# One normalisation stage between two attentions: statistics in a stage of their own, the add on GpSimd and the normalising on VectorE

## The reference, cut to what matters

```python
h = _layernorm(x, axis=-1) * (1 + ca) + sa
x = x + ga * _L0_attn_ref(h, ...)
h = _layernorm(x, axis=-1) * (1 + cb) + sb      # this line
x = x + gb * _L0_ffn_ref(h, ...)
```

## Time and profile before

| | us |
|---|---|
| median of 3 runs (4648.97, 4651.31 and 4651.40) | 4651.31 |
| the profiled execution's own time | 4651.4 |
| its span in the trace | 4649.8 |
| PE busy, share of the span | 3990.6, 86% |
| DVE busy | 3415.0, 73% |
| ACT busy | 2530.9, 54% |
| POOL busy | 1182.0, 25% |

### The profile page before, as it was taken

One profiled execution on the slowest core, in us unless ns is written; L12 is line 12 of the kernel. 1 busy time (PEld: TensorE's weight loads), 2 busy tenths in 40 slices (PEclk: granted clock), 3 DMA queues, 4 the chain that ended last, 5 costly groups with the idle time before them and its releaser, 6 DMA issues. The chain is left out here.

```text
span 4649.8 us, 98758 instructions
## 1 busy us (share of the span) xinstructions
PE 3990.6 (86%) x39612; PEld 2306.0 (50%) x39612; DVE 3415.0 (73%) x5521; ACT 2530.9 (54%) x3374; POOL 1182.0 (25%) x881
## 2 busy tenths in 40 slices
PE   7999999499969789978875999999999999726995
PEld 4788888255545445554543322332333333614664
DVE  4677778688865478865587899999989886575544
ACT  2566666455534345534323667787888887203652
POOL 1000000577840178841141000000000000312554
PEclk9999999699989889999977999999999999757998
DMA  1000000223320023220045000000000000203443
GB/s 58 1 1 1 1 1 1 58 50 56 50 60 0 9 51 55 50 54 20 0 108 94 13 11 4 11 4 3 11 3 11 4 12 8 77 0 108 95 100 95
DMA packets 289596, 157.03 MB, mean 34 GB/s; under 512 B 214704, under 2 KB 281220, under 8 KB 289156
## 3 DMA queue, kind: packets, MB, share of 16 engines
q1 hardware_dynamic: 250612, 100.68, 10.8%
q0 software_dynamic: 13440, 20.98, 2.5%
q10 hardware_dynamic: 25136, 29.64, 2.0%
HBM read 72.72 MB, written 33.55 MB: 23 GB/s over the span
## 5 line engine op out<-in xcount | busy, mean ns | idle before, releaser
L2010 DVE TENSOR_REDUCE s_tops<-ps 128x2 f32<-128x1024 f32 (+3 forms) x1152 | 1250.7, 1131 | 153.9 <-PE ps L1896 113.8
L1979 ACT ACTIVATE s_weights<-ps 128x1024 f32<-128x1024 f32 (+3 forms) x1152 | 1093.7, 953 | 344.1 <-PE ps L1909 190.1
L1931 PE MATMUL ps<-s_weights,v_flat 128*32 128x256 f32 (+1 forms) x8704 | 691.2, 389 | 7.6 <-ACT s_o_t L1985 6.2
L1890 PE MATMUL ps<-keys,s_q 48*128 48x512 f16 (+3 forms) x2304 | 433.9, 374 | 56.2 <-DVE s_tops L2010 25.9
L1909 PE MATMUL ps<-s_q,keys 50*128 50x512 f16 (+3 forms) x2304 | 433.8, 373 | 49.3 <-DVE s_tops L2010 33.2
L428 PE MATMUL ps<-a_qt,a_kt 128*128 128x256 f16 x3072 | 373.6, 273 | 3.8 <-POOL s_ones L412 3.8
L2046 POOL CAST s_shift<-s_minus_top 128x16 f16<-128x16 f32 x32 | 6.3, 198 | 1438.5 <-DVE s_minus_top L2017 1438.5
L1909 PEld LDWEIGHTS ps<-s_q,keys 50*128 50x128 f16 x2304 | 112.1, 93 | 513.6 <-issue 247.1
L929 PE MATMUL ps<-la_wqkv,la_yt 128*128 128x512 f16 x1152 | 287.8, 397 | 68.7 <-DMA la_yt<-la_y_parts 61.2
L1008 ACT ACTIVATE w_all<-ps 128x1024 f32<-128x1024 f32 x124 | 127.6, 1029 | 389.8 <-PE ps L919 389.8
L428 PEld LDWEIGHTS ps<-a_qt,a_kt 128*128 128x128 f16 x3072 | 300.0, 98 | 39.5 <-POOL s_ones L412 4.2
(11 more groups left out here) (353 smaller groups left out, 7629.6 us busy)
## 6 DMA issues: line engine op xcount, KB each, us to landing
ex_w_whole<-in_L_ffn_w_dram ACTq DMA_DIRECT2D x16, 1024.0 KB, 7.2
qk_parts<-a_parts SPq DMA_DIRECT2D x64, 128.0 KB, 2.4
keys<-qk_parts SPq DMA_DIRECT2D x48, 128.0 KB, 4.8
s_q<-qk_parts SPq DMA_DIRECT2D x48, 128.0 KB, 4.4
w_all<-in_L_ffn_wqkv_dram SPq DMA_DIRECT2D x3, 1536.0 KB, 6.4
x<-in_x_dram SPq DMA_DIRECT2D x4, 1024.0 KB, 9.5
a_table<-in_rope_dram POOLq DMA_DIRECT2D x8, 512.0 KB, 5.5
heads_out<-s_o_now SPq DMA_DIRECT2D x32, 128.0 KB, 1.9
```

Source lines behind the costliest of these rows:

```text
L1890: mm = pe.matmul(m.ps[:, bank, 0:width], b.q[rows(half, KEY_PARTS * L1_DH), place % 2, pair, t * P:(t + 1) * P], m.keys[rows(half, KEY_PAR ...
L1931: mm = pe.matmul(m.ps[h * QUAD:(h + 1) * QUAD, OUT, begin:end], m.v_flat[:, first:first + QUAD], weights[:, a % 2, h, begin:end], start=(k ...
L1979: act.activation(weights[:, a % 2, 2 * pair:2 * pair + 2, skip:CHUNK], m.ps[:, bank:end + 1, skip:CHUNK], ACT.Exp).then_inc(s["exp"], 1)
L2010: dve.tensor_reduce(tops[:, u % 2, :, i % 2, t, c], m.ps[:, bank:end + 1, 0:width], AX.X, ALU.max).then_inc(s["max"], 1)
```

## The change

The statistics leave `transformer_input` for a stage of their own, `norm_statistics(nc, m, "n1")`, right ahead of it. In `transformer_input` ACT has no work left. DVE normalises each tile with one instruction (subtract the mean, multiply by `rstd`) and multiplies the chunk. POOL adds the row, behind all its constants. The ring has 2 chunks in place of 3. The lists of DVE and POOL are loops of four rounds with two chunks in each (`in_pairs`) in place of written-out code, and their waits count from a credit of 64 that each semaphore gets at the start (`credit`, `need`).

```diff
-    FIRST, SLOTS = TPC, 3
-        normed = ctx.enter_context(nc.sbuf_tensor("y0_normed", [P, SLOTS, TPC, D], F32))
-        minus = ctx.enter_context(nc.sbuf_tensor("y0_minus", [P, TILES], F32))
+        normed = ctx.enter_context(nc.sbuf_tensor("y0_normed", [P, 2, TPC, D], F32))
...
-            @block.scalar
-            def _(act):
-                for c in range(CHUNKS):
-                    if c < 2:
-                        act.wait_ge(s["minus"], c + 1)
-                    if c >= SLOTS:
-                        act.wait_ge(s["y"], c - SLOTS + 1)
-                    for j in range(TPC):
-                        t = c * TPC + j
-                        n = act.activation(normed[:, c % SLOTS, j, :], m.x[:, t, :], ACT.Identity, bias=minus[:, t:t + 1], scale=m.rstd[:, t:t + 1])
-                    n.then_inc(s["normed"], 1)
-
             @block.vector
             def _(dve):
-                statistics_on_vector(dve, m, stats, s)
-                for n, part in enumerate(parts):
-                    dve.wait_ge(s["rstd"], n + 1)
-                    dve.scalar_tensor_tensor(minus[:, part], m.mean[:, part], -1.0, m.rstd[:, part], ALU.mult, ALU.mult).then_inc(s["minus"], 1)
-                for c in range(CHUNKS):
-                    now = normed[:, c % SLOTS, :, :]
-                    dve.wait_ge(s["normed"], c + 1)
-                    dve.tensor_tensor(now, now, m.modb[:, 4:5, :].broadcast_to([P, TPC, D]), ALU.mult).then_inc(s["scaled"], 1)
-                    dve.wait_ge(s["scaled"], c + 1)
-                    dve.tensor_tensor(m.y[:, c * TPC:(c + 1) * TPC, :], now, m.modb[:, 3:4, :].broadcast_to([P, TPC, D]), ALU.add).then_inc(s["y"], 1)
+                credit(dve, s["normed"], s["scaled"])
+
+                def norm(c, u):
+                    need(dve, s["y"], c - 1)
+                    for j in range(TPC):
+                        t = bass.ts(c * TPC + j, 1)
+                        n = dve.tensor_scalar(normed[:, u, j:j + 1, :], m.x[:, t, :], m.mean[:, t], m.rstd[:, t], ALU.subtract, ALU.mult)
+                    n.then_inc(s["normed"], 1)
+                    need(dve, s["normed"], c + 1)
+                    dve.tensor_tensor(normed[:, u, :, :], normed[:, u, :, :], m.modb[:, 4:5, :].broadcast_to([P, TPC, D]),
+                                      ALU.mult).then_inc(s["scaled"], 1)
+
+                in_pairs(dve, CHUNKS, norm)
...
             def _(pool):
+                credit(pool, s["y"])
+
                 pool.memset(m.mask[:, :, :], 0.0)
                 pool.memset(band[:, :, :], 0.0)
                 pool.memset(spread[:, :, :], 0.0).then_inc(s["zeroed"], 1)
-                pool.wait_ge(s["var"], 1)
-                for part in parts:
-                    pool.tensor_tensor(m.rstd[:, part], m.rstd[:, part], m.minus_half[:, part], ALU.pow).then_inc(s["rstd"], 1)
                 pool.wait_ge(s["zeroed"], 1)
...
                 pool.memset(m.spread[0:1, :, :], 1.0)
+
+                def shift(c, u):
+                    need(pool, s["scaled"], c + 1)
+                    pool.tensor_tensor(m.y[:, bass.ts(c, TPC), :], normed[:, u, :, :], m.modb[:, 3:4, :].broadcast_to([P, TPC, D]),
+                                       ALU.add).then_inc(s["y"], 1)
+
+                in_pairs(pool, CHUNKS, shift)
...
+            norm_statistics(nc, m, "n1")
             transformer_input(nc, m, f)
```

More of the change, by code:

```diff
@@ L599, in transformer_input @@
     NEG = -1e30
-    FIRST, SLOTS = TPC, 3
     with ExitStack() as ctx:
-        normed = ctx.enter_context(nc.sbuf_tensor("y0_normed", [P, SLOTS, TPC, D], F32))
-        minus = ctx.enter_context(nc.sbuf_tensor("y0_minus", [P, TILES], F32))
+        normed = ctx.enter_context(nc.sbuf_tensor("y0_normed", [P, 2, TPC, D], F32))
         band = ctx.enter_context(nc.sbuf_tensor("y0_band", [P, 2, P], F32))
         spread = ctx.enter_context(nc.sbuf_tensor("y0_spread", [P, 2, P], F32))
-        stats = statistics_buffers(nc, ctx, "y0")
-        with stage(nc, "y0", "table_in", "w_in", "zeroed", "selected", "spread", "minus", "normed", "scaled", "y", *STATISTICS) as (block, s):
-            parts = slice(0, FIRST), slice(FIRST, TILES)
+        with stage(nc, "y0", "table_in", "w_in", "zeroed", "selected", "spread", "normed", "scaled", "y") as (block, s):
             @block.sync
```

## The result

The changed kernel takes 4677.99 us (median of 5 runs, 4671.59 to 4684.86), the kernel before 4651.4 (median of 5, 4648.97 to 4656.73). The ratio is 1.0056, 95% interval 1.0044 to 1.0069: slower, by 20 to 32 us. A repetition in another session gave 1.0047 (1.0035 to 1.0059). The prediction, 4671.5 us or +0.43%, had the sign and most of the amount, but the median lies 2.5 us above its range. With the repetition's 1.0047 it would have lain inside (4673.2 us), so the runs alone don't tell a growth of 0.43% from a somewhat larger one. The traces do.

A forecast was written before the change was run, and what follows sets the result against it. It took the uncovered normalising stage, bound by DVE's chain, as the limit: 0.7 us at the start plus 19.5 (42.4 for 22.9) gives +20.2, so 4671.5 us (+0.43%), range 4665 to 4675.5.

The forecast's parts named there:

- What bounds the stage: Normalising stage: barriers on both sides, no other work covers it, so each microsecond it grows is one of the whole time.
- The power and the second barrier: Stage start: power ends at 844.73, the second barrier takes 1.3 us, DVE's first normalising starts at 846.0.
- GpSimd ready for shift 0: Normalising stage: POOL's constants, queued ahead of the first row add, are done and that add starts at 856.0.
- the 0.9 of turns: Constants beside DVE's first two chunks: both take 0.9 of their summed work, 9.7 us for 10.8, as in the stage before.
- Rival (a): Normalising stage: POOL's constants don't wait for DVE, POOL ready at 852.0, kernel time 4667.6 us; chance 0.10.
- the prediction's other sum: Constants by the exclusive port lock: each select and cast excludes DVE fully, POOL ready at 856.8, kernel time 4672.3 us.
- The pace from there on: Normalising stage after the first row add: six chunks (2 to 7) at 4.58 us each, 27.5 us, ending at 888.4.
- The stage as a whole: Normalising stage: its end goes from 868.17 to 888.4, +20.2 us, with the 0.8 of barrier behind it unchanged.
- The rival without exclusion (c): Normalising stage: DVE and POOL don't exclude each other, +3.5 us, kernel time 4654.9 us, within 0.2%; chance 0.07.
- the one with full turns (b): Chunk loop: DVE gets in ahead of POOL, a chunk costs 5.05 us, kernel time 4674.3 us; chance 0.07.
- es pace: Existing stage where DVE normalises beside POOL's adds and the two take turns: 4.58 us a chunk, taken over unchanged.
- rival (d): Stages behind the change: the 20 us shift alters queue meetings or clock grants, kernel time 4661 to 4682 us; chance 0.04.

The follow-up runs named there:

- the delay alone: Kernel before with 22 added ScalarE instructions on a spare buffer at the end of the normalising stage, doing nothing else; ratio 1.0043 (1.0031 to 1.0055).
- the empty stage: Kernel before with one more stage, in which no engine has work, ahead of the normalising one; ratio 1.0014 (1.0004 to 1.0024).
- the casts on ScalarE: Kernel before with GpSimd's two casts of 128x2048 and its cast of 128x256 given to ScalarE; ratio 0.9996 (0.9987 to 1.0006).

## Why the prediction was right or wrong

**What bounds the stage: right.** There was no cover, and what the stage lost the run lost: the delay alone, 18.7 us of pure waiting by the trace, made the run 1.0043 slower (20 us).

**The power and the second barrier: right.** The power ended 7.40 us behind the last statistics (forecast 7.43), and the first normalising started at 9.05 (forecast 8.7).

**GpSimd ready for shift 0: forecast 1.8 us too late.** The forecast was 18.7 us behind the last statistics; it was 855.80 - 838.91 = 16.9. Two terms of the sum were mis-sized in opposite ways. A cast of 2048 alone takes 3.73 / 2 = 1.87, not 1.65. But the 0.9 of turns, taken from a stretch in which VectorE ran long instructions without a pause, was too much. In the changed kernel the two casts went through back to back in 3.79, as good as alone, and VectorE's group took 4.55 in place of 1.38: two of its four instructions 0.41, and two, one beside each cast, 2.01 and 1.98. In the run with the add on VectorE the casts took 4.66, as the first started at 850.91, while an addition on VectorE ran until 851.92. So a cast does wait behind a two-input instruction that is already running. Why none of the normalising instructions held up the second cast stays open. Rival (a), constants that don't wait for VectorE, was half right: GpSimd was ready midway between its 14.7 us and the forecast's 18.7. By the exclusive lock of the Trainium skill's page "SBUF — State Buffer", section "SBUF: two separate sides", the prediction's other sum had GpSimd ready still later, so that sum was further off. The exclusion itself is seen here, in the 2.01, 1.98 and 2.44 us for 0.40, but it needn't delay GpSimd.

**The pace from there on: right.** 4.59 measured for 4.58. From the first shift to the end of the last there were 888.84 - 855.80 = 33.0 us for 32.4 forecast; the first pair of shifts took 5.19.

**The stage as a whole: right.** It grew by 19.06 for 20.2 forecast. The rival without exclusion (c) and the one with full turns (b) are out: the pace was the es pace. Of the forecast's 5.2 us for the constants' place ahead of shift 0, the run with the constants last showed 3.6. The add back on VectorE, with groups of 1.38 and 3.9 us a chunk, shows GpSimd's adds as the cause of the pace.

**The later stages: the step that failed.** The prediction made the run's growth equal to the stage's, and called the rest rival (d) with a chance of 0.04. The loop was 1451.9 us on the mean of two profiles for 1443.7 of three: 8.2 more. With the stage that makes 27.3, or 1.0059 of the run, which lies in the first interval and at the end of the second (1.0059); 19.06 alone is 1.0041, under the first interval but inside the second. Nothing in the diff touches the loop, and the empty stage, with none of the change's work, has the whole of it. What makes the loop longer stays open.

Where in the loop it lies can be told in part. By the start times, two profiles against three, 1.9 us lie in the first layer ahead of its MLP, 1.2 at the loop's turn, 2.1 in the second layer ahead of its MLP, 2.4 in the two MLPs together and 0.5 at the end. The view of waits at the loop's turn (who waited for what, total us, times, longest), before and then after, shows GpSimd starting the second layer from "issue", a wait for nothing that the profile shows, where it was a barrier before:

```profile
POOL la_yt L821 <- POOLq L81: 45.9, 1, 45.9
ACT L998 <- issue: 15.5, 1, 15.5
```

```profile
POOL la_yt L815 <- issue: 50.4, 1, 50.4
ACT L992 <- issue: 16.6, 1, 16.6
```

GpSimd is 4.6 us late there, but ScalarE's first conversion, for which VectorE waits, sets the path, and that comes 1.2 us later (its table load starts 5.7 us behind the last work of the first layer for 4.5). The late GpSimd isn't what the long loops share: only the four kernels with the shifts on GpSimd have it, the one with written-out lists among them, and the empty stage, with a loop of 1451.9, has the barrier wait of before. It goes with another row, that of the DMA packets of kind "instruction" (queue, packets, MB, share), before and after:

```profile
q14 instruction: 116, 0.95, 0.1%
```

```profile
q14 instruction: 121, 0.99, 0.1%
```

Those four kernels have 120 or 121 of these packets and all others, with long loops or short, 116 or 117.

TensorE's clock differs in the first 40 us of each of the two MLP stages. The windows of the third profile of before, and of after:

```profile
1379.60:1419.60 40.00, 33.06 (x184) 19.16 (x185) 21.13 (x43) 15.54 (x26) 7.34 (x3) 0.85 0.18 55
2103.40:2143.40 40.00, 33.06 (x184) 19.17 (x185) 21.22 (x44) 15.53 (x26) 7.34 (x3) 0.85 0.18 55
```

```profile
1400.50:1440.50 40.00, 33.06 (x179) 18.97 (x180) 20.15 (x40) 14.82 (x25) 7.33 (x3) 0.82 0.19 55
2128.30:2168.30 40.00, 33.00 (x181) 19.05 (x182) 20.50 (x41) 15.07 (x26) 7.36 (x3) 0.83 0.20 55
```

The granted clock goes up from its 1.2 GHz level a little later (0.82 and 0.83 in the mean for 0.85), fewer matmuls are done, and the MLP takes 210.9 and 210.6 us for 208.2 and 208.1. But this comes and goes in the kernel before too: in its other two profiles the MLP was 208.2 once in four, and the repeated one, with the shortest loop of all (1442.6), had 211.2 and 210.2. So the clock isn't what tells a long loop from a short one.

The whole-run ratios agree with stage plus loop within their intervals, the repeated change at the upper end of its own, but for the casts on ScalarE: -2.1 + 7.5 would be 1.0012, and 0.9996 (to 1.0006) was measured. So a single profile's loop isn't each run's.

## What to carry to other kernels

If the same pair of engines already does the same two steps elsewhere in the trace, take the pace from there: it held to 0.01 us in 4.58. Freeing an engine that isn't the limit gains nothing. Giving VectorE's work to GpSimd gained nothing either, since the two took turns here: 1.23 us of VectorE's add became 2.0 us of waiting. An edit that adds or moves a few instructions ahead of a long loop can change the loop by several us with nothing to see in the diff, so a forecast finer than about 0.15% of this kernel needs that in its range.

## What the runs showed of the hardware that was not expected

Five semaphore increments on one engine, in a stage that they didn't lengthen, went with a loop 2 to 5 us longer behind it, whichever of four engines had them (1446.0 to 1449.0 for 1442.6 to 1444.4). Between GpSimd's casts and VectorE's normalising the turns were one-sided: two casts took 3.79 us beside VectorE and 3.73 alone, while beside VectorE's long two-input instructions they took 5.59. And an instruction of VectorE that met a GpSimd instruction stood still as a whole: 2.44 us for 0.40 beside a shift of 2.34.
